# Experts and the second projection in one loop of frames, with the second attention behind it in the same block

## What is computed

```python
# first layer, feed-forward: 16 routed experts of 64 (top 4 by group) and one shared expert of 128
combine = (one_hot(idx, E) * weights[..., None]).sum(1)
g = silu(einsum('th,efh->tef', x, w1_e)); u = einsum('th,efh->tef', x, w3_e)
routed = einsum('tef,ehf,te->th', g * u, w2_e, combine)
shared = (silu(x @ w1_s.T) * (x @ w3_s.T)) @ w2_s.T
...
# second layer, attention: 8 heads, queries and keys of 64, values of 128, heads summed
Q = (x @ Wq.T).reshape(b, n, 8, 64); K = (x @ Wk.T).reshape(b, n, 8, 64)
V = (x @ Wv.T).reshape(b, n, 8, 128)
attn = softmax(einsum('bnhr,bmhr->bhnm', Q, K))
out = einsum('bhnm,bmhd->bnd', attn, V)
```

## Time and profile before

| | us |
|---|---|
| median of three runs | 2271.17 (2267.74 to 2271.22) |
| the profiled execution, its own time | 2272.57 |
| its span from first to last instruction | 2270.8 |
| TensorE busy | 2006.3 (88%) |
| VectorE busy | 1628.7 (72%) |
| ScalarE busy | 1346.2 (59%) |
| GpSimd busy | 1106.4 (49%) |
| mean granted TensorE clock | 0.945 of full |

### The profile page before, as it was taken

One profiled execution on the slowest core, in us unless ns is written; L12 is line 12 of the kernel. 1 busy time (PEld: TensorE's weight loads), 2 busy tenths in 40 slices (PEclk: granted clock), 3 DMA queues, 4 the chain that ended last, 5 costly groups with the idle time before them and its releaser, 6 DMA issues. The chain is left out here.

```text
span 2270.8 us, 56437 instructions
## 1 busy us (share of the span) xinstructions
PE 2006.3 (88%) x17787; PEld 1021.1 (45%) x17787; DVE 1628.7 (72%) x3429; ACT 1346.2 (59%) x2148; POOL 1106.4 (49%) x999
## 2 busy tenths in 40 slices
PE   5689999999999999974899659999999999998576
PEld 3434444444444444444444214444444444443355
DVE  4978888888888888868566866666666666664696
ACT  2246666666666666542555537777778787877121
POOL 1412322223222232504455318878778787877465
PEclk8889999999999999986999979999999999999787
DMA  5612222112211122100000560111111011100000
GB/s 133 187 48 52 54 53 50 49 52 54 53 50 49 53 54 53 38 11 0 1 0 0 171 181 29 33 38 28 42 28 42 28 42 28 42 14 1 1 14 24
DMA packets 127021, 106.80 MB, mean 47 GB/s; under 512 B 39636, under 2 KB 102724, under 8 KB 126956
## 3 DMA queue, kind: packets, MB, share of 16 engines
q1 hardware_dynamic: 120544, 99.83, 16.5%
q10 hardware_dynamic: 6412, 6.18, 1.0%
HBM read 76.01 MB, written 29.53 MB: 46 GB/s over the span
## 5 line engine op out<-in xcount | busy, mean ns | idle before, releaser
L1099 DVE TENSOR_REDUCE b_mx<-psum 128x1 f32<-128x512 f32 x1024 | 664.0, 687 | 140.3 <-PE psum L916 76.9
L1083 ACT ACTIVATE b_prob<-psum 128x1024 f32<-128x1024 f32 x512 | 524.4, 1024 | 319.2 <-PE psum L948 319.1
L1851 POOL TENSOR_TENSOR f_plo<-f_prob,f_phi 128x512 f16<-128x512 f32 x512 | 586.7, 1157 | 164.5 <-ACT f_phi L1976 139.8
L1994 DVE TENSOR_REDUCE f_mx<-psum 128x1 f32<-128x512 f32 x512 | 328.7, 683 | 169.4 <-PE psum L1871 168.3
L1975 ACT ACTIVATE f_prob<-psum 128x512 f32<-128x512 f32 x512 | 307.3, 600 | 151.0 <-PE psum L1882 149.9
L996 PE MATMUL psum<-b_prob,combT 128*32 128x256 f32 x4096 | 328.3, 392 | 1.5 <-ACT b_prob L1083 0.5
L852 POOL COPY combT<-v 128x64 f32 (+1 forms) x64 | 15.7, 245 | 606.9 <-PE psum L996 597.6
L1976 ACT ACTIVATE f_phi<-psum 128x512 f16<-128x512 f32 x512 | 305.4, 597 | 0.0
L948 PE MATMUL psum<-x,b_toep 128*128 128x79 f16 (+1 forms) x4224 | 267.1, 208 | 0.0
L855 POOL TENSOR_TENSOR x<-flip,grev 128x1024 f16<-128x1024 f16 x128 | 240.5, 1899 | 0.0
L948 PEld LDWEIGHTS psum<-x,b_toep 128*128 128x128 f16 x4224 | 235.5, 99 | 9.1 <-issue 2.6
(11 more groups left out here) (312 smaller groups left out, 3419.7 us busy)
## 6 DMA issues: line engine op xcount, KB each, us to landing
d_qk<-e_qk SPq DMA_DIRECT2D x64, 256.0 KB, 2.7
b_toep<-d_line SPq DMA_DIRECT2D x128, 64.0 KB
f_qa<-d_qk SPq DMA_DIRECT2D x64, 128.0 KB, 2.9
f_ka<-d_qk SPq DMA_DIRECT2D x64, 128.0 KB, 2.9
b_q<-d_q SPq DMA_DIRECT2D x128, 54.0 KB
d_k<-a_qk SPq DMA_DIRECT2D x48, 128.0 KB, 2.4
b_toep<-d_line SPq DMA_DIRECT2D x128, 32.0 KB
b_q<-b_m SPq DMA_DIRECT2D x256, 1.0 KB
```

Of the source, the lines that this page charges most:

```text
L1083: nc.scalar.activation(prob[:, t % 4, :].rearrange("p (a n) -> p a n", a=2), ps[:, EXP + 2 * (t % 2):EXP + 2 * (t % 2) + 2, :], ACT.Exp).t ...
L1099: nc.vector.tensor_reduce(mx[:, b, t, half:half + 1], ps[:, bank, :], AX.X, ALU.max).then_inc(s.max_read, 1)
L1851: nc.gpsimd.tensor_tensor(plo[:, t % 4, at], prob[:, t % 4, at], phi[:, t % 4, at], ALU.subtract).then_inc(s.plo_ready, 1)
L1994: nc.vector.tensor_reduce(mx[:, b, t, half:half + 1], ps[:, MAX + half, :], AX.X, ALU.max).then_inc(s.max_read, 1)
```

## The change

1. The turning and copying of the last stage's weights moves from the head of phase_project1 to the head of phase_route, in banks 5 to 7, ahead of the wait for VectorE's ranking.
2. phase_experts and phase_project1 become one phase of ten frames. Frame n holds the units of chunk n, the output, its add, statistics and normalisation of chunk n-1, and the turn and eight products (four pairs, `project`) of chunk n-2. GATE and UP are given in turn to the fourteen places of a frame (FRAME). Frames 0 and 1 have no projection, frames 8 and 9 no units.
3. Unit tiles lie in wT, which is not used any more by then; prob and plo of the attention lie in g.attn and combT.
4. phase_attend1 runs in the same block behind the frames. Batch b's first load is issued behind the stores of its own chunks: the sync engine issues the stores of chunks 0 to 3, then waits for those of 0 and 1, loads batch 0, issues the stores of chunks 4 and 5, and so on. TensorE waits for the last product, unit, add and kept x before the first score; GpSimd waits for the last kept x before it clears f_kb.

And in the routing and the attention:

```diff
@@ phase_route, tensor
+                for i in range(2):
+                    for c, (x, y) in enumerate(FC):
+                        at = (i * len(FC) + c) * P
...
+                ins.then_inc(w_turned, 1)
                 pe.wait_ge(ready, 1)
+                pe.wait_ge(w_moved, 1)
@@ phase_attend1
-        prob = sb("f_prob", [P, 4, N])
+    prob = g.attn[:, :, :].rearrange("p t e -> p (t e)").rearrange("p (i n) -> p i n", i=4)
...
-        plo = sb("f_plo", [P, 4, N], F16)
+    plo = g.combT[:, :].rearrange("p (i n) -> p i n", i=4)
@@ sync
                 for b in range(B):
                     sp.sem_inc(m_stored[b], 32)
-                    load(0, b)
+            before.stored_chunks(sp, 2 * b + 2)
+            load(0, b, True)
+            for n in {0: (4, 5), 1: (6, 7)}.get(b, ()):
+                before.store(sp, n)
@@ gpsimd
+        pool.wait_ge(before.xt_kept, done(NC - 1))
@@ tensor
+        pe.wait_ge(before.qk_lo, done(before.last_product))
+        pe.wait_ge(before.hid_ready, done(before.last_unit))
+        pe.wait_ge(before.out_added, done(NC - 1))
+        pe.wait_ge(before.xt_kept, done(NC - 1))
```

More of the change, by code:

```diff
@@ L1331, in phase_route @@
         dchain, ready, turned = sem("r_dchain"), sem("r_ready"), sem("r_turned")
+        w_turned, w_moved = sem("r_w_turned"), sem("r_w_moved")
+        W_BANKS = (5, 6, 7)
         ps = g.ps
@@ L1409, in _ @@
             def _(pe):
[L1410 to L1420, removed]
@@ L1687, in _ @@
                 ins.then_inc(w_turned, 1)
-                def turn_x(n, u):
-                    pe.wait_ge(s.xn_ready, done(n))
-                    pe.wait_ge(s.xT_low, done(n - 2))
+                pe.wait_ge(ready, 1)
+                pe.wait_ge(w_moved, 1)
+                for c in range(NC):
                     for k in range(CT):
-                        last = nc.tensor.transpose(ps[:, TX + u, k * P:(k + 1) * P], ln.xn[:, u, k, :], g.ident[:, :])
-                    last.then_inc(s.x_turned, 1)
@@ L1696, in project @@
-                def project(n, u, products):
-                    pe.wait_ge(s.xT_low, done(n))
-                    x = [g.x16[:, part, bass.ds(n * CHUNK, CHUNK)] for part in range(2)]
-                    for i in products:
-                        if i == RING - 1:
-                            pe.wait_ge(w_moved, 1)
-                        pe.wait_ge(s.lo_ready, done(M * n + i - RING))
-                        product16(nc, ps[:, QK + i % RING, :], g.w16[:, :, IN_16[W_Q1 + i], :], x).then_inc(s.qk_psum, 1)
@@ L1947, in _ @@
+                        ins = nc.tensor.transpose(ps[0:2 * NE, c, k * P:(k + 1) * P], parts[:, c * CT + k, :], g.ident[:, :])
+                    ins.then_inc(turned, 1)
             @block.scalar
             def _(act):
-                credit(act, s.exp_ready, s.m_hi, s.y_hi)
-                def move_m(h, b):
-                    act.wait_ge(s.m_turned, done(4 * h + b))
-                    act.wait_ge(m_stored[(b + 2) % 4], 32 * (h + b // 2 + 1))
-                    nc.scalar.copy(m16[:, b % 2, 0, :], ps[0:TB, M_BANK, 0:P]).then_inc(s.m_hi, 1)
@@ new lines, in _ @@
+                act.wait_ge(w_turned, 1)
+                for i in range(2):
+                    nc.scalar.copy(g.wguT[:, i, :], ps[:, W_BANKS[i], 0:FI])
+                for c, (x, y) in enumerate(FC):
+                    ins = nc.scalar.copy(g.wdT[0:y - x, c, :], ps[0:y - x, W_BANKS[2], c * P:(c + 1) * P])
+                ins.then_inc(w_moved, 1)
+                for c in range(NC):
+                    act.wait_ge(turned, c + 1)
+                    nc.scalar.copy(g.combT[0:2 * NE, c * CHUNK:(c + 1) * CHUNK], ps[0:2 * NE, c, :])
@@ L2311, in program @@
         phase_route(nc, g, a)
-        phase_experts(nc, g, a)
-        phase_project1(nc, g, a)
-        phase_attend1(nc, g, a)
+        with ExitStack() as both, nc.Block() as block:
+            before = phase_experts(nc, g, a, both, block)
+            phase_attend1(nc, g, a, both, block, before)
         phase_quant_ffn(nc, g, a, out)
```

938 lines of the change are left out of this document (439 added, 499 removed).

## The result

The kernel after takes 2265.3 us (median of 20 runs, 2254.4 to 2309.1), the kernel before, in the same rounds, 2273.1. Ratio 0.995, 95% interval 0.9927 to 0.9973. (The ratios here leave disturbed runs out; the medians don't.) Forecast were 2246 us, 1.1% faster, range 2235 to 2263. The sixteen undisturbed times of after fall in two groups, ten from 2254.4 to 2261.7 and six from 2268.8 to 2282.2. The profiled execution, 2268.8 us, is of the second.

What follows compares the result with a forecast made beforehand. Experts and attention were taken as bound by TensorE, with 79.6 + 11.2 us between them not. First maximum from 1343.7 to 1318.7 saves 25.0: 2272.6 - 25.0 = 2247.6, median 2246 us; own range 2238 to 2256, 8 in 10: 2235 to 2263.

Steps and rivals of the forecast that it cites:

- no instruction of the steady attention is altered: Second attention: its instructions stay the same, so its windows were to stay unchanged at 708 us.
- My bounds for the attention: Second attention: temporary tiles in other tensors might change its 708 us by 0.5%, 3.5 us both ways.
- The frames: Joined experts and projection: frames 2 to 7 were to take 27.2 us each, against 20 in the first.
- The wait that I worked out at 0.7: In each frame: TensorE stalls 0.7 us before unit 8, behind VectorE's burst of output addition and statistics.
- The two stalls that I added: In each frame: 0.3 us for normalisation before projection 3 and 0.4 for queueing on ScalarE.
- my 1.4: Frames 2 to 7: total TensorE stall per frame, 0.7 + 0.3 + 0.4 us.
- the 20.02: Experts in the earlier trace: period of one chunk in us, to which each projection adds 5.82 of TensorE.
- rival E: In frames: each of four normalisations waits out a GpSimd subtraction, 25 us more in all, 2271; chance 0.03.
- E: End of the last expert matmul: 1250.8 us in the earlier trace, forecast at 1292.6.
- Rival C: In frames: shared banks tie TensorE to VectorE, 7 us stall a frame, 34 us more, 2280; chance 0.10.
- The tail: Frames 8 and 9: from the last expert matmul to the last low part, forecast 24 us.
- rival B: Burst and normalisation cost 3 to 4 us a frame, tail 28; 2263; chance 0.12 together with another rival.

Runs made afterwards that it cites:

- e1: Kernel after with 154 more satisfied waits on ScalarE ahead of the second attention's loop; 2248.5 us, ratio 0.9899 to the kernel before.
- e2: Kernel after with 40 more satisfied waits on ScalarE ahead of the second attention's loop; 2257.7 us, ratio 0.9922 to the kernel before.
- e3: Kernel before with 101 more satisfied waits on ScalarE ahead of the second attention; 2284.1 us, ratio 1.0043.
- e4: Kernel before with only the change's temporary tiles (prob in g.attn, plo in g.combT); 2275.2 us, ratio 1.0005.
- e12: Kernel before with 120 satisfied waits on TensorE ahead of the first attention's loop; 2272.3 us, ratio 0.9969.
- e9: e5 with the stores of chunks 6 and 7 ahead of batch 1's load on SyncE; 2242.4 us, ratio 0.9841 to the kernel before.
- e5: e2 with 120 more satisfied waits on TensorE ahead of the first attention's loop; 2246.0 us, ratio 0.9877 to the kernel before.
- e7: Kernel after with 128 more satisfied waits on ScalarE ahead of the second attention's loop; 2261.6 us, ratio 0.9941 to the kernel before.
- e6: e2 with 25 more satisfied waits on TensorE ahead of the first attention's loop; 2348.2 us, ratio 1.0330 to the kernel before.
- e11: e5 with the second attention in its own block again, all stores before it and loads behind; 2250.6 us, ratio 0.9875 to the kernel before.

## Why the prediction was wrong

**The step that failed** is "no instruction of the steady attention is altered", from which it took "The attention's windows unchanged at 708 us". The first half is true. The second doesn't follow: the time of a loop also hangs on its place in the engine's program, and the prediction had no term for that. It cost 9.1 us (742.8 for 733.7 to the last addition; e1 and e2 get it back), and e3 shows the cause without the change. Of the 19 us by which the measured median is over the forecast this is about half; the rest is in the next paragraph. My bounds for the attention, 3.5 us both ways, were tied to the tiles, which e4 puts at nothing.

**The base.** The forecast started from 2272.6, a profiled execution without a late jump of TensorE, and by its time the median of 2271.2 is one too. Ten runs of after seem to be so (2254 to 2262); 2246.2 + 9.1 = 2255.3 is their place. Five of the other six are 13 to 15 us above that place, as is the profiled one with its two late jumps (the first attention 13.1 longer). The prediction had no term for this either, and the kernel before meets it as well. The runs without a trace can only be assigned by their times, and they differ without late jumps too: the profiled executions of before and of e12 have none and are 4.3 us apart.

**The frames.** Forecast 27.2 us. Output additions of frames 2 and 5 of after, timeline of VectorE:

```profile
1158.52 0.68 DVE L1733 TENSOR_TENSOR x<-x,psum 128x512 f32 x1
...
1237.18 0.68 DVE L1733 TENSOR_TENSOR x<-x,psum 128x512 f32 x1
```

Three periods, 26.22 us each. The wait that I worked out at 0.7, for the burst of addition and statistics, is there. It is TensorE's only one in a frame:

```profile
1188.18 0.39 PE L382 MATMUL psum<-x,w 128*128 x1 [0.77 <-DVE e_qk L1752]
```

The matmul starts 1.15 us behind the one before instead of 0.22, so it costs 0.93. The two stalls that I added, for normalisation and for queueing on ScalarE, don't exist, which takes 0.5 off my 1.4. Another 0.4 is a wait of TensorE for GpSimd in each chunk of the experts, which is part of the 20.02 and is gone in the frame (in before a matmul of each chunk starts 0.60 behind the one before, where 0.22 is the time). The last 0.2 is a reading: four transposes take 0.65 to the end of the last one, but the next matmul starts 0.43 after the first, so the earlier trace rows should give 5.6 us for a projection chunk and not 5.82.

Four normalisations took 1.11 us in frames 2 to 6, less than the 1.83 of the earlier trace rows, and GpSimd stood idle while they ran. Where it was at work they did wait. VectorE and GpSimd at the end of frame 7:

```profile
1297.05 1.96 DVE L364 TENSOR_SCALAR e_xn<-x,e_mv,e_rstd 128x128 f32<-128x128 f32 x4
```

```profile
1297.01 1.16 POOL L1685 TENSOR_TENSOR wT<-wT 128x512 f16<-128x512 f32 x1 [0.79 <-ACT wT L1631]
```

The first of the four took 1192 ns and ended within 0.1 us of GpSimd's subtraction, the others 335 each. In frame 1 two of four took 1122 and 1195 ns, each beside one subtraction, and the four 2.75 us. The other 29 of the 32 took about 339. So of rival E, in which every normalisation waits out a subtraction, the waiting is real, but it is rare: in frames 2 to 6 GpSimd has nothing to do at that moment. The Trainium skill's rule ("SBUF — State Buffer", section "Who interferes with whom"), by which the one that comes second is blocked for the whole instruction, agrees with these three. The prediction took such waits for a slowness of all four together, between 1.83 and 2.80; in the four of the earlier trace rows too it is one that took 1057 ns.

E came 197.9 us after the start of the stretch (the last down starts at 1298.64 and shows 0.38) where I had 202.7: 4.8 too many, which is what six frames 1.0 us too long make (6.1), less 1.3 elsewhere. Rival C was far off.

**The tail.** From E to the last low 27.9 us, not 24. Timelines of after, SyncE, ScalarE and VectorE:

```profile
1301.44 0.47 SPq L1850 DMA_DIRECT2D f_qa<-d_qk  x1
...
1305.15 22.18 SPq L1514 DMA_DIRECT2D d_qk<-e_qk  x16
```

```profile
1311.16 0.59 ACT L1654 CAST e_qk<-psum 128x512 f16<-128x512 f32 x1 [6.14 <-DMA d_qk<-e_qk]
```

```profile
1325.58 1.35 DVE L1752 TENSOR_TENSOR e_qk<-psum,e_qk 128x512 f16<-128x512 f32 x2 [0.67 <-ACT e_qk L1654]
1327.25 2.10 DVE L2082 MEMSET f_qb<- 64x512 f32 x4 [0.32 <-issue]
1329.39 2.08 DVE L2044 TENSOR_REDUCE f_mx<-psum 128x1 f32<-128x512 f32 x3
```

The mechanism was named (batch 1's six issues ahead of the stores, a ring of four), its price not: the stores leave 3.7 us late, ScalarE's copies stand 6.1 us for them, and on VectorE and TensorE the normalisation and turn of chunk 7 stand behind those copies, so one late store delays both last chunks. I charged 1.5. e9, without it, has the last low at E + 21.5; I had said 21 without the loads. The tail of 28 is rival B's, which I took for the price of slow landings. The clear of `f_qb` took its 2.1 us, the first maximum came 2.5 after the last low for 2.1, and the first exponential 18.0 us after the first maximum, as forecast. That 228.8 and 228.3 look alike is luck: errors of opposite sign, -4.8 in the frames and +3.9 and +0.4 behind them, cancelled.

With the fetches out of the way (ScalarE's in e1, both engines' in e5) the change reaches 2248.5 and 2246.0, where the forecast was. The sum that gave it has terms that are off by 4 to 5 us each way.

## What to carry to other kernels

A loop that is kept word for word can change its time when code ahead of it on the same engine grows. Look at the instruction queues of the page and at the first instruction behind each loop's jump, and compare the two kernels; "waits for PE" may be the engine fetching its own code. Where a jump is late, some tens of satisfied waits ahead of the loop, in a place where the engine idles, settle it and may cure it. They may also do harm: on TensorE 120 instructions cured the loop, and 25 made it 100.7 us longer. So look at the jumps again after every such change.
A load placed early on a queue that also carries the stores of a short ring costs the ring. Ask when it is wanted and put it behind the stores if that is soon enough.

## What the runs showed of the hardware

- ScalarE: a loop of 288 instructions jumps back in at most 0.28 us at three of the places tried (before, e1, e2) and in 2.4 to 2.7 at the others (after, e3, e7), two of which lie 128 instructions apart. The second attention loses 1.5 us a pass to it in after (9.1 in six; 9.3 in e3, 10.9 in e7); the rest falls into idle time of ScalarE.
- TensorE: a loop of 1625 instructions jumps back in 0.3 us or less, or in 3.7 to 5.2; with the clock that it loses behind it (0.94 in e6's first attention, 0.99 in e5's), a late jump costs 7.2 us (e6: 100.7 us for 14). At the place it has in both kernels, four of eight profiled executions had one or two late jumps, always among the first four, then none. 25 instructions on, all are late; 120 on, none in five profiles. Why it is chance at the first place, and why it stops after some passes, stays open.
- VectorE: a `tensor_scalar` of 128x128 took about 339 ns with GpSimd idle, and 1122 to 1195 where it met a GpSimd subtraction of 1.16 us (three of 32 in after, and the same three in e1, e2, e5, e7, e9 and e11).
